# The last attention of a four-stage kernel: dividing by the softmax sums in another layout, and where the output projection runs

## What is computed

```python
qkv = (x @ W_qkv).reshape(Bx, Nx, 3, H, D)          # H = 16 heads of D = 16
logits = jnp.einsum('bqhd,bkhd->bhqk', q * scale, k)
def masked_attn(tok_mask):
    key_mask = jnp.concatenate([jnp.ones((Bx, REG), bool), tok_mask], axis=1)
    l = jnp.where(key_mask[:, None, None, :], logits, -jnp.inf)
    return jnp.einsum('bhqk,bkhd->bqhd', jax.nn.softmax(l, axis=-1), v)
x_pos, x_neg = masked_attn(pos), masked_attn(~pos)
reg_out = (x_pos[:, :REG] + x_neg[:, :REG]) * 0.5   # the 5 register tokens
tok_out = jnp.where(pos[:, :, None, None], x_pos[:, REG:], x_neg[:, REG:])
out = jnp.concatenate([reg_out, tok_out], axis=1).reshape(Bx, Nx, Cx) @ W_proj + b_proj
```

## Time and profile before

| | us |
|---|---|
| median of 3 runs | 1333.91 (1333.17 to 1338.76) |
| profiled execution, its own time | 1333.7 |
| span of the profiled execution | 1332.0 |
| busy in the span: PE, DVE, ACT, POOL | 1215.1, 1000.7, 835.3, 227.5 |
| mean granted clock of PE | 0.965 of full speed |

### The profile page before, as it was taken

The page is one execution under the profiler, slowest core; times in us unless marked ns, Lnnn a source line. Parts: engine busy times, 40 slices in busy tenths (PEclk is TensorE's granted clock), DMA queues, the critical chain, the costliest instruction groups (busy, mean ns, idle before and its releaser), DMA issues.

```text
span 1332.0 us, 26359 instructions
## 1 busy us (share of the span) xinstructions
PE 1215.1 (91%) x10562; PEld 565.5 (42%) x10562; DVE 1000.7 (75%) x1491; ACT 835.3 (63%) x1484; POOL 227.5 (17%) x176
## 2 busy tenths in 40 slices
PE   4989974999999898879999999999999999999988
PEld 3566762555567455343233232332232333333247
DVE  4895695665536758368999999999999999999602
ACT  1224573777742742115887878887788877888861
POOL 2130124554741423710000000000000000000000
PEclk9878985999999999888999999999999999999989
DMA  6100027557500334722323443144332543233003
GB/s 189 26 1 15 1 31 137 121 108 136 96 1 1 119 119 135 134 35 48 56 62 64 87 72 63 47 82 84 56 68 56 87 78 59 56 70 50 2 1 126
DMA packets 78825, 92.55 MB, mean 69 GB/s; under 512 B 15210, under 2 KB 53356, under 8 KB 78704
## 3 DMA queue, kind: packets, MB, share of 16 engines
q1 hardware_dynamic: 78704, 90.87, 33.7%
HBM read 67.02 MB, written 23.80 MB: 68 GB/s over the span
## 4 chain that ended last, share of the span: by engine, by line
PE 60%; DVE 27%; ACT 5%; issue 2%; SPq 2%; DMA 2%; POOL 1%; DVEq 0%; ACTq 0%; POOLq 0%
DVE sm L2093 19%; PE ps L1560 10%; PE ps L1551 9%; PE ps L1532 6%; ACT W L1022 3%; PE ps L1322 2%; PE ps L1670 2%; PE ps L1416 2%; PE ps L1313 2%; PE ps L1314 2%; PE ps L1375 2%; PE ps L1542 1%; PE ps L1280 1%; PE ps L1278 1%; PE ps L1331 1%
## 5 line engine op out<-in xcount | busy, mean ns | idle before, releaser
L1022 ACT ACTIVATE W<-ps 128x512 f32<-128x512 f32 x1024 | 534.8, 605 | 140.6 <-PE ps L1560 136.7
L2093 DVE TENSOR_REDUCE sm<-ps 128x1 f32<-128x1024 f32 x512 | 599.3, 1217 | 29.7 <-PE ps L1532 26.3
L1560 PE MATMUL ps<-R 99*32 99x512 bf16 x4096 | 319.2, 384 | 5.5 <-ACT W L1022 3.2
L1551 PE MATMUL ps<-W,R 128*32 128x512 f32 x2048 | 265.5, 594 | 0.7 <-ACT W L1022 0.7
L1560 PEld LDWEIGHTS ps<-R 99*32 99x32 bf16 x4096 | 86.1, 94 | 225.2 <-ACT W L1022 167.0
L803 POOL COPY R<-R 128x512 f32<-128x512 f32 x16 | 9.7, 613 | 629.5 <-PE ps L1551 625.9
L1532 PE MATMUL ps<-R 50*128 50x512 bf16 x512 | 89.9, 390 | 17.7 <-DVE sm L2093 15.0
L1532 PE MATMUL ps<-KM,R 50*128 50x512 bf16 x512 | 87.3, 384 | 9.6 <-DVE sm L2093 6.6
L945 ACT ACTIVATE R<-ps 77x512 f32<-77x512 f32 x128 | 75.1, 592 | 23.5 <-PE ps L1314 14.2
L1551 PEld LDWEIGHTS ps<-W,R 128*32 128x32 f32 x2048 | 63.0, 111 | 42.2 <-ACT W L1022 1.4
L1872 DVE TENSOR_REDUCE small<-ps 128x4 bf16<-128x308 f32 x128 | 57.5, 472 | 23.2 <-PE ps L1280 23.1
(11 more groups left out here) (262 smaller groups left out, 1576.0 us busy)
## 6 DMA issues: line engine op xcount, KB each, us to landing
R<-x_parts SPq DMA_DIRECT2D x96, 128.0 KB, 4.8
R<-q_parts SPq DMA_DIRECT2D x192, 64.0 KB
R<-q_parts SPq DMA_DIRECT2D x96, 128.0 KB
R<-k_parts SPq DMA_DIRECT2D x96, 128.0 KB
x_parts<-R SPq DMA_DIRECT2D x8, 768.0 KB, 7.0
q_parts<-R SPq DMA_DIRECT2D x24, 256.0 KB, 2.6
k_parts<-R SPq DMA_DIRECT2D x24, 256.0 KB, 2.6
X<-in_x SPq DMA_DIRECT2D x4, 1024.0 KB, 9.8
```

The costliest lines, as they stand in the source:

```text
L1022: act.activation(PR[:, s % 2, h, :], third_bank("score", 64 * u + n), ACT.Exp, scale=0.25).then_inc(s_sfree, 1)
L1551: mm = pe.matmul(bank(7)[32 * h:32 * h + 32, :], VST[j][:, k, h, :], PR[:, s % 2, h, :], start=(k == 0), stop=(k == TB - 1))
L1560: mm = pe.matmul(o[32 * c:32 * c + 32, :], KST[j][0:MAX_ROW + 1, h, t:t + 32], QST[j][0:MAX_ROW + 1, h, 512 * (s // 8):512 * (s // 8) + 51 ...
L2093: dve.tensor_reduce(MX[:, half, h, q:q + 1], bank(2 * ((p + 1) % 2), 2), AX, ALU.max).then_inc(s_tfree, 1)
```

## The change

The output of a unit stays with its channels on partitions. ACT's copy of bank 7 is sorted by five DMAs per half (`sort_out`): four move the 16 rows of each head to their place in `OT2`, one writes the four rows of sums to DRAM. When two units (128 channels of a batch) have been collected, their sums are loaded as 128x32 per half (`load_sums`), inverted by DVE (`invert_sums`, before tile 24 of the even unit that follows), stored (`store_factors`), spread over 16 partitions each (`spread_factors`, 256 KB), and POOL multiplies 128x512 (`divide_out`). The out turns, `normalise2` and the transposes and copies of the end are gone. The register average runs on `OT2`, for the first three batches before the last unit, for the last batch near the end. The projection (`project2`, one call for 128 tokens) takes its operand from `OT2`: 14 of its 32 calls run in the steps of the last unit, in the banks that the tiles have left, and 18 behind it. The last call group (chunk 7) waits for the last division. The sum over registers in the prologue gives its result transposed (two products of 5 columns). Some semaphores are shared.

```diff
...
+        DN = nc.dram_tensor("sum_rows", (2, 2, 8, 512), F32).ap()
+        DR = nc.dram_tensor("sum_factors", (2, 2, 8, 512), F32).ap()
...
-        On2 = R1[:, :].rearrange("p (k u n) -> p k (u n)", u=UNITS, k=TB)
+
+        OT2 = R1[:, :].rearrange("p (j b t) -> p j b t", j=2, b=B)
...
+        Den2 = [W[:, 4096:4608], XNf[:, 1152:1664]]
+        Rd2 = XNf[:, 1664:1728].rearrange("p (u n) -> p u n", u=2)
...
         PLAN = [[("tile", n)] for n in range(32)]
         PLAN[2].insert(0, ("rows", 1))
         PLAN[18].insert(0, ("rows", 0))
-        PLAN[20].insert(0, ("out", 0))
-        PLAN[30].insert(0, ("out", 1))
-        PLAN_LAST = [[] for _ in range(32)] + [[("out", 1)]]
+        PLAN_LAST = [[] for _ in range(32)]
         PLAN_LAST[2].append(("rows", 1))
...
+            def sort_out(u, half):
+                b, rows, j = u // 4, 64 * (u % 2), u // 2 % 2
+                sp.wait_ge(s_oe2, 2 * u + half + 2)
+                for h in range(4):
+                    v = slice(rows + 16 * h, rows + 16 * h + 16)
+                    sp.dma_start(OT2[v, j, b, 512 * half:512 * half + 512],
+                                 Oe2[32 * h:32 * h + 16, half, :]).then_inc(s_od2[half], 16)
+                sp.dma_start(DN[u // 2 % 2, half, 4 * (u % 2):4 * (u % 2) + 4],
+                             Oe2[16:P:32, half, :]).then_inc(s_od2[half], 16)
+
+            def load_sums(k, half):
+                sp.wait_ge(s_od2[half], 80 * (2 * k + 2))
+                if k >= 1:
+                    sp.wait_ge(s_nd2, 2 * (k - 1) + half + 1)
+                sp.dma_start(Rd2[:, half, :],
+                             DN[k % 2, half].rearrange("g (a n) -> (g a) n", a=16)).then_inc(s_dd2[half], 16)
+
+            def store_factors(k, half):
+                sp.wait_ge(s_rc2, B + 2 * k + half + 1)
+                sp.dma_start(DR[k % 2, half].rearrange("g (a n) -> (g a) n", a=16),
+                             Rd2[:, half, :]).then_inc(s_dd2[half], 16)
+
+            def spread_factors(k, half):
+                sp.wait_ge(s_dd2[half], 48 * k + 32)
+                sp.dma_start(Den2[half], DR[k % 2, half].unsqueeze(1).to_broadcast([8, 16, 512])
+                             ).then_inc(s_dd2[half], 16)
+
+            def store_out(c):
+                sp.wait_ge(s_x3, NC + c + 1)
+                sp.dma_start(out[c // 2].rearrange("(i p) c -> p i c", p=P)[:, 4 * (c % 2):4 * (c % 2) + 4, :],
+                             X[:, 4 * c:4 * c + 4, :]).then_inc(s_out, 16)
+
             def body_sp(u, j, last=False, load=True):
                 store_row(j, 1, s_bfree, small_turn(u, "rows", 1) + 1, u)
                 if load:
                     load_max_stacks(u + 2, j)
+                if u >= 3 and u % 2 == 1:
+                    for half in range(2):
+                        store_factors((u - 3) // 2, half)
+                sort_out(u, 0)
+                if u >= 2:
+                    for half in range(2):
+                        if u % 2 == 0:
+                            load_sums((u - 2) // 2, half)
+                        else:
+                            spread_factors((u - 3) // 2, half)
                 if not last:
                     store_row(1 - j, 0, s_bfree, small_turn(u, "rows", 0) + 1, u + 1)
+                else:
+                    load_sums(UNITS // 2 - 1, 0)
+                    store_out(0)
+                    store_factors(UNITS // 2 - 1, 0)
+                    spread_factors(UNITS // 2 - 1, 0)
+                    for c in range(1, 3):
+                        store_out(c)
                 if load:
                     sp.wait_ge(s_sco, 64 * (u + 1))
                     load_stacks(u + 2, j)
+                sort_out(u, 1)

             for u in range(UNITS):
                 body_sp(u, u % 2, last=u + 1 == UNITS, load=u + 2 < UNITS)
-            for c in range(NC):
-                sp.wait_ge(s_x3, NC + c + 1)
-                sp.dma_start(out[c // 2].rearrange("(i p) c -> p i c", p=P)[:, 4 * (c % 2):4 * (c % 2) + 4, :],
-                             X[:, 4 * c:4 * c + 4, :]).then_inc(s_out, 16)
+            load_sums(UNITS // 2 - 1, 1)
+            store_factors(UNITS // 2 - 1, 1)
+            spread_factors(UNITS // 2 - 1, 1)
+            for c in range(3, NC):
+                store_out(c)
...
+            def divide_out(k, half):
+                pool.wait_ge(s_od2[half], 80 * (2 * k + 2))
+                pool.wait_ge(s_dd2[half], 48 * (k + 1))
+                o = OT2[:, k % 2, k // 2, 512 * half:512 * half + 512]
+                pool.tensor_tensor(o, o, Den2[half], ALU.mult).then_inc(s_nd2, 1)
+
+            for u in range(UNITS):
+                if u >= 3 and u % 2 == 1:
+                    for half in range(2):
+                        divide_out((u - 3) // 2, half)
+                if u + 2 < UNITS:
+                    pool.wait_ge(s_pv2, 2 + 16 * (u + 1))
+                    stage_values(u + 2, u % 2)
+            for half in range(2):
+                divide_out(UNITS // 2 - 1, half)
+

...
             def copy_out2(u, half):
                 act.wait_ge(s_pv2, 16 * u + 8 * half + 10)
+                if u >= 1:
+                    act.wait_ge(s_od2[half], 80 * u)
...
-                    turns(plan[32])
+
+            def project2(i):
+                c, q = i // 4, i % 4
+                n = NC + c
+                if i == 0:
+                    pe.wait_ge(s_tfree, PAIRS0 + 32 * (UNITS - 1))
+                    pe.wait_ge(s_avg, 2)
+                if i == 4 * (NC - 2):
+                    pe.wait_ge(s_avg, 4)
+                if i == 4 * (NC - 1):
+                    pe.wait_ge(s_nd2, UNITS)
+                if q == 0 and c >= 2:
+                    pe.wait_ge(s_x3, n - 1)
+                o = bank(2 * (c % 2) + q // 2)[:, C * (q % 2):C * (q % 2) + C]
+                for j in range(2):
+                    mm = pe.matmul(o, OT2[:, j, c // 2, 512 * (c % 2) + P * q:512 * (c % 2) + P * q + P],
+                                   wproj[:, j, :], start=(q % 2 == 0 and j == 0), stop=(j == 1),
+                                   skip_group_check=True)
+                if q == 3:
+                    mm.then_inc(s_wo, 1)


             pe.sem_inc(s_pv2, 2)
...
-            pe.wait_ge(s_avg, 1)
-
-            def transposes2(c):
...
-                mm.then_inc(s_wo, 1)
+            for i in range(14, NT):
+                project2(i)
...
+            def invert_sums(k, half):
+                dve.wait_ge(s_dd2[half], 48 * k + 16)
+                dve.reciprocal(Rd2[:, half, :], Rd2[:, half, :]).then_inc(s_rc2, 1)
...
                 n = PAIRS0 + TURNS * u
                 for what, arg in sum(PLAN_LAST if last else PLAN, []):
                     if what == "tile":
+                        if arg == 24 and u >= 2 and u % 2 == 0:
+                            for half in range(2):
+                                invert_sums((u - 2) // 2, half)
                         reduce_tile(n, PAIRS0 + 32 * u + arg, arg)
                     else:
-                        o = third_bank("small", small_turn(u, what, arg))
...
+            def average_registers(batches):
+                for j in range(2):
+                    o = OT2[:, j, batches, 0:REG]
+                    dve.scalar_tensor_tensor(o, o, 0.5, regT[:, j, batches, :], ALU.mult, ALU.add).then_inc(s_avg, 1)
+
+            def x4_chunk(c):
+                dve.wait_ge(s_wo, NC + c + 1)
+                dve.wait_ge(s_xb, B + c // 2 + 1)
+                xs = X[:, 4 * c:4 * c + 4, :]
+                dve.scalar_tensor_tensor(xs, bank(2 * (c % 2), 2).rearrange("p (i n) -> p i n", i=4),
+                                         gates[:, 3:4], xs, ALU.mult, ALU.add).then_inc(s_x3, 1)
+
             for u in range(UNITS):
+                if u + 1 == UNITS:
+                    dve.wait_ge(s_nd2, 4 * (B - 1))
+                    average_registers(slice(0, B - 1))
                 body_dve(u, last=u + 1 == UNITS)
-
-            dve.wait_ge(s_bfree, small_turn(UNITS - 1, "out", 1) + 1)
-            dve.scalar_tensor_tensor(On2[0:REG, 0, :], On2[0:REG, 0, :], 0.5,
-                                     regn.rearrange("p b c -> p (b c)"), ALU.mult,
-                                     ALU.add).then_inc(s_avg, 1)
-            for c in range(NC):
-                dve.wait_ge(s_wo, NC + c + 1)
-                dve.wait_ge(s_xb2, c // 2 + 1)
-                xs = X[:, 4 * c:4 * c + 4, :]
-                dve.scalar_tensor_tensor(xs, bank(4 + 2 * (c % 2), 2).rearrange("p (i n) -> p i n", i=4),
-                                         gates[:, 3:4], xs, ALU.mult, ALU.add).then_inc(s_x3, 1)
+            x4_chunk(0)
+            invert_sums(UNITS // 2 - 1, 0)
+            for c in range(1, 3):
+                x4_chunk(c)
+            dve.wait_ge(s_nd2, UNITS - 1)
+            average_registers(slice(B - 1, B))
+            for c in range(3, 5):
+                x4_chunk(c)
+            invert_sums(UNITS // 2 - 1, 1)
```

(42 more changed lines are left out.)

81 lines of the change are left out of this document (17 added, 64 removed).

## The result

| | before | after |
|---|---|---|
| median of the runs beside each other, us | 1334.03 (4 runs, 1333.17 to 1338.76) | 1296.82 (4 runs, 1295.72 to 1301.07) |
| profiled execution: own time, span, us | 1333.7, 1332.0 | 1296.1, 1294.3 |
| mean granted clock of PE | 0.965 | 0.961 |

The ratio after to before is 0.9721, with a 95% interval of 0.9695 to 0.9748: 2.8% faster. The forecast was 1291.2 in a range of 1285 to 1301; the median is 5.6 us above it and inside the range.

A forecast was written before the change was run, and what follows sets the result against it. PE and DVE, both nearly full and handing banks back and forth, were taken as the bound. The terms -28.5 + 3.5 + 7.8 - 25.3 = -42.5 us took 1333.7 to 1291.2 us, range 1285 to 1301 with the late end.

The forecast's parts named there:

- all four terms: The nonzero parts of the predicted sum: output turns -28.5, reciprocals +3.5, last unit +7.8, end -25.3 us.
- the term in the units: From the first row turn to the last maximum: output turns and reciprocals, -28.5 + 3.5 = -25.0 us.
- (a): Units 0 to 14: two output turns each disappear, 30 x 0.95 = -28.5 us.
- (b): Units 2, 4, ... 14: two 128x32 reciprocals on DVE, 0.72 us per event, 0.5 counted, +3.5 us.
- (c): POOL's 128x512 divisions, two per two units, about 1.15 us each: no cost and no slowing of DVE, 0.
- (d): SP's queue: 13 new DMAs a unit at 0.35 us per issue, bound 0.6, fit its waits: 0.
- (e): Last unit: 14 projection groups of 0.865 us make PE the bound, steps 2.78 us, last copy +7.8 us.
- (f): From the last copy to the end: 20.6 us instead of 45.9, with a 12.4 us chain to chunk 7, -25.3.
- Late end: PE waits for chunk 7, chain 3 us late and clock falls: 1297.7 us, chance 0.22.
- Half the gain: Worse hand-over phase between PE and DVE, a removed turn worth only about 0.5 us: 1304.7 us, chance 0.07.
- SP: SP becomes the bound as small DMAs hold its queue, from 1.7 us each; at 2.0, 1349 us, chance 0.03.
- Nothing gained: A wait of equal size replaces the turns and the end's DMA chain is 12 us late: 1332 us, chance 0.01.

The follow-up runs named there:

- The pairs: Two projection groups in every second step of the last unit instead of one in each, against the changed kernel: 1300.32 us (one run).

## Why the prediction was right, and where it was off

**The direction and most of the size**: all four terms came within 1.7 us. The profiled time was 4.9 us above the forecast (1296.1 against 1291.2): +2.9 ahead of the units, -1.4 in them, +1.6 in the last unit, +1.7 behind it. Some of the closeness is luck: the term in the units was off the other way than the two behind it. The largest part of the miss, ahead of the units, stood in no term.

**(a) Output turns, -28.5.** 42.48 - 40.57 = 1.91 per unit, 0.955 a turn, 30 of them: -28.7. Right, as it was read from the pace and not from the instructions. Behind the 0.95 the prediction put DVE's wait of 0.67 us; the runs show 0.60 of it to be PE's transposes.

**(b) Reciprocals, +3.5.** They took 0.55 us a pair and cost 0.30 each time (40.88 against 40.57), 0.43 the first time, 2.2 in all. The choice "nearer the full price as DVE is nearly full" was wrong: about half of the 0.55 went into DVE's holes of 0.27 us. What made the first time dearer was not looked into.

**(c) POOL, 0.** 1.28 us a division where I had 1.15, and POOL is busy 2.1 of 40.6 us in a unit with divisions. DVE's maxima kept their 4.73 us per four. Right.

**(d) SP, 0.** Right in the sum, wrong in its size: a head row was issued in 0.59 us, not 0.35 (the bound was 0.6), and in the excerpt of waits SP waited for a row turn only once in two units. I had taken the price from copies of 4 and 8 KB; the stack loads in the same queue of before took 0.53 us each (12 from L594 in 6.37 us, from 751.32). A second effect was not foreseen: a row of maxima landed 3.9 us after its issue (median), before 1.4, and SP waited 11.1 us for the rows in two units instead of 5.0. The rows came later and PE did not wait for them, here and with ten more DMAs, so they had that much slack.

**(e) The last unit, +7.8.** It was +9.4. The term that was mis-sized is "A group is 3.46 / 4 = 0.865 us on PE": in a step it is 1.06. The pairs show 0.19 saved where two groups follow each other. The starts in the trace split it: the first product of a group is followed by the next after 0.32 us instead of 0.22, and the last one by the scores after 0.31. The weight loads of this line are 190 ns long and begin 0.1 us behind the product before them inside a run; the first load of the group (1264.06) and the first of the scores behind it (1265.12) begin with their own product. A step's own work was 1.84, not 1.91, so the two errors partly cancel: 2.90 instead of 2.78, 13 times. The first group started 0.3 us behind the last maximum, as worked out.

**(f) The end, -25.3.** It was -23.6. The chain took 13.9 us instead of 12.4: the four issues 2.5 (I had 1.4), the spread of 256 KB 4.0 (3.3); the other hops were 1.5 to 1.8 as taken. PE waited 1.65 us instead of 0.3. The sizes of the hops were misread as 16 and 32 KB; they are 8, 16 and 16 KB. The clock did not fall: it was 1.00 from 1286 to 1290. The stores behind the spread did not push the last one; it landed 3.3 us behind the addition. The Trainium skill ("DMA: Bandwidth & Descriptors", Anatomy of one DMA) has some 2.0 us fixed per DMA, for DMAs that GpSimd issues. These came from SP: the small hops took 1.5 to 1.8 us, the one of 256 KB 4.0, 9.0 in all, where the estimate from the page is 8.6. The parts don't fit the page, so the nearness of the sums says little.

**The rivals.** Late end: its mechanism exists (2.08 us of waiting and a clock of 0.69 in one variant, 4.55 and 0.52 in another). In the changed kernel PE waited 1.65 us and the clock stayed at 1.00, as it did behind a wait of 2.17 in another variant, so that this end was on time is partly luck. Half the gain: no, plain pairs kept 5.01. SP: not at 13 DMAs a unit of up to 0.6 us, and at 23 it cost 2.5 us in 14 units. Nothing gained: no such wait was there.

**Ahead of the units, +2.9**: not a term of the sum; I had the new register sum at "no cost". Its own time on PE fits that; what lengthens the stretch stays open, as told above.

## What to carry to other kernels

In a loop where two engines are both full, read what an extra step costs from the pace of the loop with and without it, and ask which engine's instructions it is made of: here matmuls cost their full time, and some changes of kind 0.1 us more, while short work on the other engine vanished in part into holes. Look which changes of kind cost and keep those products together, as long as no other engine becomes the bound: paired projections saved 0.19 us of PE and lost more than that to ACT's pace. At the end of a kernel follow the chain of small DMAs through both queues it passes: what is issued ahead of the critical one, and what the receiving engine has been told to do first. Here mending one of the two gave nothing.

## What was not expected of the hardware

- Some changes of kind cost PE time even with no wait: the products of two tiles in one run 0.53 us, of one alone 0.32; a group of four f32 projections 0.865 us in a run and 1.06 between scores. Between scores (99\*32) and values (128\*32) a change costs nothing, though their types and rows differ. The Trainium skill ("TensorE: Matmul & The Clock Gate", Part 3, The mechanism) says that the weights of a product are loaded while earlier ones run if they go to other row groups or into the background buffer. In a run of projections, all on 128 rows, the 190 ns loads did lie beside the 216 ns matmuls (16 in 3.46 us); behind the score matmuls the first did not. Why is not shown.
- A DMA of 2 KB from each of 16 partitions to 16 others took SP 0.59 us to issue (median), one of four such rows to DRAM 0.53, one of 4 KB from 16 partitions to DRAM 0.33.
- PE waits of 1.65, 1.76 and 2.17 us left the granted clock in the next chunk as it was (3.72 us), one of 2.08 did not (5.41 us); so the wait's length alone does not tell.
